# An LSTM step on one core: VectorE's transposes and the new cell in PSUM, the cell copied back to SBUF

## What is computed

```python
xW = jnp.einsum('ntd,dg->ntg', x, Wx) + b
def step(carry, xw_t):
    prev_h, prev_c = carry
    a = xw_t + prev_h @ Wh                 # Wh: 256 x 1024
    i = sigmoid(a[:, :H]); f = sigmoid(a[:, H:2*H]); o = sigmoid(a[:, 2*H:3*H])
    g = tanh(a[:, 3*H:])
    next_c = f * prev_c + i * g
    next_h = o * tanh(next_c)
    return ((next_h, next_c), next_h)
x = x + scan(step, (h0, 0), xW)            # 1024 steps, each needs the one before
ys = cond * scale
d = rsqrt((ys * ys) @ (weight * weight) + EPS)
x = x + ((x * ys) @ weight) * d
```

## Time and profile before

| | |
|---|---|
| time, median of 3 runs | 2266.88 us (2264.55 to 2268.80) |
| the profiled execution's own time | 2266.96 us |
| its span, first to last instruction | 2265.2 us |
| mean granted TensorE clock | 0.997 of full speed |
| VectorE busy | 1410.6 us, 62% of the span |
| ScalarE busy | 860.6 us, 38% |
| TensorE busy | 1564.2 us, 69% |
| steps | 1024 |

### The profile page before, as it was taken

The page is one execution under the profiler, slowest core; times in us unless marked ns, Lnnn a source line. Parts: engine busy times, 40 slices in busy tenths (PEclk is TensorE's granted clock), DMA queues, the critical chain, the costliest instruction groups (busy, mean ns, idle before and its releaser), DMA issues.

```text
span 2265.2 us, 121696 instructions
## 1 busy us (share of the span) xinstructions
PE 1564.2 (69%) x50018; PEld 1255.0 (55%) x50018; DVE 1410.6 (62%) x12341; ACT 860.6 (38%) x4117; POOL 117.7 (5%) x651
## 2 busy tenths in 40 slices
PE   6666676676666766666666666666666676676666
PEld 5555555555555555555555555555555555555555
DVE  5666666666666666666666666666666666666665
ACT  3333333333333333333333333333333333333333
POOL 0000000000000000000000000000000000000000
PEclk9999999999999999999999999999999999999999
DMA  1000000000000000000000000000000000000000
GB/s 51 4 7 6 3 9 3 7 6 3 9 3 7 6 3 9 4 7 6 3 9 3 7 6 3 9 3 9 3 4 9 3 9 4 4 9 3 7 3 5
DMA packets 7278, 15.31 MB, mean 7 GB/s; under 512 B 1649, under 2 KB 6129, under 8 KB 6642
## 3 DMA queue, kind: packets, MB, share of 16 engines
q1 hardware_dynamic: 5824, 5.64, 0.9%
q10 hardware_dynamic: 818, 1.05, 0.1%
HBM read 4.59 MB, written 2.10 MB: 3 GB/s over the span
## 4 chain that ended last, share of the span: by engine, by line
DVE 46%; PE 35%; ACT 10%; issue 8%; DMA 0%; DVEq 0%; SPq 0%; POOL 0%; POOLq 0%
PE pA L266 35%; DVE turned L399 29%; DVE junk L405 11%; ACT gates L213 10%; DVE hst L414 5%; DVE gates L405 1%; DMA wx_sb<-in_L_cond_Wx_dram 0%; ACT tanhc L218 0%; PE pX L243 0%; DVE xT L352 0%; PE pA L255 0%; PE pX L289 0%; DVEq L388 0%; SPq L111 0%; PE pA L252 0%
## 5 line engine op out<-in xcount | busy, mean ns | idle before, releaser
L266 PE MATMUL pA<-wh_sb,hst 128*2 128x128 f32 (+3 forms) x40960 | 1096.6, 252 | 687.7 <-DVE hst L414 644.4
L266 PEld LDWEIGHTS pA<-wh_sb,hst 128*2 128x2 f32 (+1 forms) x40960 | 795.6, 90 | 966.1 <-DVE hst L414 913.2
L399 DVE STREAM_TRANSPOSE turned<-pA 128x128 f32<-128x128 f32 x2048 | 647.8, 317 | 592.7 <-PE pA L266 579.7
L213 ACT ACTIVATE gates<-turned 128x8 f32<-128x8 f32 x2048 | 442.0, 216 | 1259.2 <-DVE turned L399 1144.5
L405 DVE CUSTOM_DVE_ANT_0 junk<-gates 128x4 f32<-128x4 f32 x4096 | 504.6, 160 | 75.4
L218 ACT ACTIVATE tanhc<-gates 128x2 f32<-128x2 f32 x2048 | 418.3, 204 | 127.9 <-DVE gates L405 0.8
L414 DVE TENSOR_TENSOR hst<-tanhc,gates 128x2 f32<-128x2 f32 x2048 | 330.6, 161 | 169.6 <-ACT tanhc L218 162.8
L243 PE MATMUL pX<-wh_sb,ones 128*32 128x128 f32 x2416 | 419.1, 274 | 0.0
L405 DVE DVE_READ_ACCUMULATOR2_ANT gates<- 128x1 f32 x4096 | 336.1, 82 | 0.0
L243 PEld LDWEIGHTS pX<-wh_sb,ones 128*32 128x32 f32 x2416 | 265.2, 111 | 4.7 <-issue 2.7
L255 PE MATMUL pA<-wx_sb,xblk 128*16 128x128 f32 x4128 | 207.9, 274 | 0.0
(11 more groups left out here) (32 smaller groups left out, 39.1 us busy)
## 6 DMA issues: line engine op xcount, KB each, us to landing
xin<-in_x_dram SPq DMA_DIRECT2D x34, 64.0 KB, 2.1
out_dram<-ores SPq DMA_DIRECT2D x32, 64.0 KB, 2.5
wh_sb<-in_L_cond_Wh_dram ACTq DMA_DIRECT2D x1, 1024.0 KB, 8.9
wx_sb<-in_L_cond_Wx_dram SPq DMA_DIRECT2D x1, 1024.0 KB, 9.0
w_sb<-in_L_cond_weight_dram SPq DMA_DIRECT2D x1, 256.0 KB, 3.4
condT<-in_cond_dram ACTq DMA_DIRECT2D x2, 1.0 KB, 2.2
bias_sb<-in_L_cond_b_dram ACTq DMA_DIRECT2D x1, 4.0 KB
```

The costliest lines, as they stand in the source:

```text
L213: act.activation(gates[:, j, :, 0:3 * G:3].rearrange("p b g -> p g b"), turned[:, j, :, B * t:B * (t + 1)], ACT.Sigmoid).then_inc(gates_re ...
L266: last = pe.matmul(pA[st][j][c * Q:c * Q + M, lo * Q:hi * Q].rearrange("p (g u) -> p g u", u=Q), hst[:, st, k, Q * t:Q * t + M], chunk(wh_ ...
L399: dve.transpose(turned[:, j, :, :].rearrange("p g r -> p (g r)"), pA[blk % SETS][j][:, 0:P]).then_inc(turned_ready[j], 1)
```

## The change

Two more PSUM tiles of that size, `pT0` and `pT1`, are added. The transpose of half j writes columns 0 to 127 of its `pT`, in place of the SBUF tile `turned`, and the sum of the cell goes to the two columns behind them (`cells[j]`), in place of column `AT_C` of `gates`. ScalarE's sigmoid and tanh read from these. As the next step reads the old cell out of `gates`, VectorE copies it there, two instructions of 128x2 for each step, behind both products. The number of steps, all of TensorE's work and the order of everything else stay as they are.

```diff
-        turned = sb("turned", [P, K, G, Q])
+        pT = [ctx.enter_context(nc.psum_tensor(f"pT{j}", [P, 512], F32)) for j in range(K)]
+        turned = [pT[j][:, 0:G * Q].rearrange("p (g r) -> p g r", g=G) for j in range(K)]
+        cells = [pT[j][:, G * Q:G * Q + B] for j in range(K)]
...
                         act.activation(gates[:, j, :, 0:3 * G:3].rearrange("p b g -> p g b"),
-                                       turned[:, j, :, B * t:B * (t + 1)], ACT.Sigmoid).then_inc(gates_ready[j], 1)
+                                       turned[j][:, :, B * t:B * (t + 1)], ACT.Sigmoid).then_inc(gates_ready[j], 1)
...
-                        act.activation(tanhc[:, j, :], gates[:, j, :, AT_C], ACT.Tanh, scale=2.0).then_inc(tanh_ready[j], 1)
+                        act.activation(tanhc[:, j, :], cells[j], ACT.Tanh, scale=2.0).then_inc(tanh_ready[j], 1)
...
-                        dve.transpose(turned[:, j, :, :].rearrange("p g r -> p (g r)"),
+                        dve.transpose(pT[j][:, 0:G * Q],
                                       pA[blk % SETS][j][:, 0:P]).then_inc(turned_ready[j], 1)
...
-                                accum_out=gates[:, j, b, AT_C:AT_C + 1])
+                                accum_out=cells[j][:, b:b + 1])
...
+                    for j in range(K):
+
+                        dve.wait_ge(cell_ready[j], i + (ls + 1))
+                        dve.tensor_copy(gates[:, j, :, AT_C], cells[j])
```

## The result

The changed kernel takes 2322.99 us (median of 4 runs, 2319.25 to 2326.77), the kernel before 2266.28 us (median of 4). The ratio is 1.0249, 95% interval 1.023 to 1.0269. The forecast of 2218 us was wrong, in sign too; the time fell close to the upper end that the prediction had worked out for its slower rival, 2326 us.

What follows compares the result with a forecast made beforehand. The recurrence's two half loops, meeting at TensorE, were taken as the bound. 2267.0 us less 54.3 (1024 steps of 53 ns) plus 5 for copies gave 2218 us; the 8-in-10 range was 2185 to 2285.

Steps and rivals of the forecast that it cites:

- slower rival: At the ends of transpose and accumulator read, VectorE loses what ScalarE saves or more; 2272 to 2326 us, chance 0.15.
- What bounds the kernel: The recurrence: two half loops meeting at TensorE, 2.15 us a step; half 0 without slack, half 1 with 0.01 us.
- Part 1: ScalarE's sigmoid and tanh reading PSUM: about 35 and 32 ns shorter, 67 ns a step in each half's loop.
- Part 2: VectorE's transpose and cell sum writing PSUM: effect called unknown, taken as 6 ns more per write from its reads.
- it counts twice: The added write cost enters each half's loop at the transpose's end and at the accumulator read that releases tanh.
- d: What writing to PSUM adds to a VectorE instruction: taken as +6 ns, possible from -32 to +60.
- The 65 ns: VectorE's SBUF to PSUM gap, 58 against 120 cycles; applied to both writes it would give about 2336 us.
- three limits: Step gain is the least of 67 - 2d, 61 - d and 59 - d; 53 ns for d = +6.
- The two limits: On VectorE's queue, cell 0 behind transpose 1 caps the gain at 61 - d, product 0 behind cell 1 at 59 - d.
- Part 3: VectorE's two copies behind product 1: 0.24 us, hidden in nearly all steps; if exposed, 246 us in all.
- The 5 us for restarts and step 2: Copies uncovered at 15 loop restarts and in 16 second steps of a loop body, up to 0.16 us each.
- the accumulator read shows over 110 ns: A sign that would prove the forecast wrong; the cell's accumulator read was expected at 82 + d, d near 6.

Runs made afterwards that it cites:

- the first experiment: The changed kernel with the cell's unread products (junk) in PSUM too, so both instructions of a cell write PSUM; 2230.18 us, ratio 0.982 against the kernel before.

## Why the prediction was wrong

- **What bounds the kernel** was right: the step's two loops, no slack in half 0. Adding up the changed durations along half 0 gives +53 ns, the median step grew by 54.
- **Part 1, ScalarE's gain** was right: 32 and 32 ns, where 35 and 32 stood. Its support was thinner than the text says: one line drawn through a sqrt and a tanh can't show that both have the same fixed part. The two results show it after the fact, with source and function told apart: tanh is 32 ns shorter out of PSUM, and so is the sigmoid.
- **Part 2, VectorE's write to PSUM, failed.** The step that failed is "it counts twice", one price d for both writes, taken as +6 from the reads. Two numbers were behind it. A plain write to PSUM costs 10 to 15 ns more: transpose 317 to 332, a cell whose writes all go there 254 to 264. The other is no price of a write but of an order: the cell is four writes, and the edit moved two of them, so that they alternate. That cost 102 ns where 6 stood. The text ahead of the prediction notes that the cell is two instructions for each row, but of the four outputs the prediction followed only the sums; the unread products that stayed in SBUF weren't costed at all.
- **The range for d** reached +60 from above, and the sum of both writes came to 15 + 102 = 117, by chance just under twice 60. So the time of the slower rival, 2326, was near 2323. Its mechanism, "VectorE pays for PSUM what ScalarE saves, or more", is not what happened: with every write of a cell in PSUM the kernel is 1.8% faster than before. The rule of the Trainium skill that stood beside it ("Advanced Engine Details and Errata", the read-write bubble, VectorE closer to SBUF) holds in direction for writes, by 10 to 15 ns. The 65 ns that the prediction set beside it come from the Trainium skill's table in "VectorE: DVE Perf Modes", section on the TRN2 errata, which gives them for a source in PSUM, not for an output there; for sources the trace shows no such thing either, a 128x2 copy out of PSUM taking 153 ns (the page above) where one out of SBUF took 165. Had d been +12 for both, the least of the three limits (43, 49 and 47 ns a step) would have put the time near 2228; the first experiment, which has just that, measured 2230.
- **The two limits** (cell 0 behind transpose 1, product 0 behind cell 1) never came into play in the changed kernel, where product 0 starts 93 ns after cell 1's last read has. In the first experiment the second was just reached, with a distance of 0 ns, and cost nothing; with tanh in PSUM it delayed the product by 16 ns, 48 ns from tanh's end in place of 32.
- **Part 3, the copies** was right: hidden in each normal step. The 5 us for restarts and step 2 can't be told from what the restarts vary by; step 2 itself lost nothing, its median is 2.197 us.
- **The signs named beforehand** pointed the right way: "the accumulator read shows over 110 ns" was the one that came true.

The range ended at 2285 and gave 0.19 to slower. The rows could not have given the 102 ns: in the kernel before, all small writes of VectorE went to one memory. They could have given the question, since the edit made outputs alternate that hadn't, and nothing in the trace priced that.

## What to carry to other kernels

When the output of a VectorE instruction moves between SBUF and PSUM, look at what the instructions right before and behind it write, unread outputs included, and move them together; check the ends in the timeline, not the starts, since the starts don't change. A small intermediate that VectorE writes and ScalarE reads was better off in PSUM here: 32 ns saved on each read against 10 to 15 lost on each write. In a chain of short instructions each price has to be asked for each output, not for each statement of the code.

## What the runs showed that I had not expected

- Of two VectorE instructions in a row with outputs in different memories, the later one ended 57 to 60 ns after the earlier where it wrote to SBUF and 65 to 68 ns where it wrote to PSUM (medians, wherever it would otherwise have ended sooner). An accumulator read took 142 ns behind an instruction to the other memory, 185 if that one was delayed itself, 82 with all in SBUF, 92 with all in PSUM. The start of the later one isn't delayed. Why the end waits wasn't shown.
- The delay is caught up: one switch at the head of a cell left the kernel at a ratio of 1.0007 (0.9997 to 1.0016).
- It doesn't show where the two ends lie that far apart anyway: in the first experiment the product of half 0, into SBUF, started together with the last read, into PSUM, still took 0.16 us and ended 69 ns after it.
- VectorE's writes to PSUM cost 10 ns (small ones) to 15 ns (the transpose) more than to SBUF; ScalarE's cost 14 ns less.
